# VectorE turns the probabilities of all four tiles, layernorm units later, four heads' scores and the second tile's rows moved

## The reference

```python
xn = layernorm(x)
q, k, v = (xn @ W + b  for each of q, k, v), as (blocks of 64 tokens, 8 heads, 128)
probs = softmax(q @ k.T * 128**-0.5)          # 64 x 64 for a head of a block
x = x + (probs @ v) @ Wo + bo
h = square(relu(layernorm(x) @ W_fc.T))
y = h @ W_proj.T
x = x + spikes(y) / 5                         # 5 steps of a leaky threshold: a count of y's levels
```

## Time and profile before

| | |
|---|---|
| median of 3 runs | 707.44 us (707.12 to 707.58) |
| the profiled execution's own time | 707.24 us |
| span of its slowest core (core 5), first to last instruction | 705.6 us |
| spans of the eight cores | 702.7 to 705.6 us |
| TensorE busy | 691.9 us, 98% |
| VectorE busy | 390.9 us, 55% |
| ScalarE busy | 179.7 us, 25% |
| granted TensorE clock, mean | 0.997 to 0.999 of full |

### The profile page before, as it was taken

One profiled execution on the slowest core, in us unless ns is written; L12 is line 12 of the kernel. 1 busy time (PEld: TensorE's weight loads), 2 busy tenths in 40 slices (PEclk: granted clock), 3 DMA queues, 4 the chain that ended last, 5 costly groups with the idle time before them and its releaser, 6 DMA issues.

```text
span 705.6 us, 10623 instructions; the slowest of 8 cores (702.7 to 705.6 us)
## 1 busy us (share of the span) xinstructions
PE 691.9 (98%) x3772; PEld 323.3 (46%) x3772; DVE 390.9 (55%) x589; ACT 179.7 (25%) x330; POOL 49.7 (7%) x96
## 2 busy tenths in 40 slices
PE   7999999999999999999999999999999999999996
PEld 3544444444444444444444444444444444444444
DVE  5327863776687488337655227845225865221476
ACT  3544550460351135130003331002331002332000
POOL 2211110211005000000000000000000000000000
PEclk9999999999999999999999999999999999999998
DMA  8998996598669995496461002272002152000011
GB/s 182 210 152 148 160 163 185 117 218 202 157 180 204 247 209 93 145 168 182 122 177 60 1 1 61 67 202 89 1 1 61 37 142 88 32 0 2 30 46 46
DMA packets 31012, 80.94 MB, mean 115 GB/s; under 512 B 5616, under 2 KB 5872, under 8 KB 30192
## 3 DMA queue, kind: packets, MB, share of 16 engines
q0 software_dynamic: 12960, 31.46, 26.0%
q1 hardware_dynamic: 15552, 40.39, 20.3%
q10 hardware_dynamic: 2448, 8.40, 3.0%
HBM read 82.33 MB, written 16.78 MB: 140 GB/s over the span
## 4 chain that ended last, share of the span: by engine, by line
PE 93%; DMA 4%; DVE 1%; issue 1%; POOL 0%; DVEq 0%; POOLq 0%
PE ps_m L439 31%; PE ps_y L517 30%; PE ps_m L386 13%; PE ps_m L412 8%; PE ps_m L426 8%; DMA wq_sb<-Wq 4%; DVE acc_sb L785 1%; PE ps_y L466 1%; PE ps_y L499 1%; PE ps_m L524 0%; PE ps_t L478 0%; DVE acc_sb L782 0%; DVE xr L790 0%; PE ps_t L368 0%; POOL wq_sb L879 0%
## 5 line engine op out<-in xcount | busy, mean ns | idle before, releaser
L439 PE MATMUL ps_m<-xn2t,w_sb 128*128 128x512 bf16 x1024 | 222.3, 379 | 0.0
L517 PE MATMUL ps_y<-w_sb,h_sb 128*128 128x512 bf16 (+1 forms) x1024 | 218.3, 376 | 0.0
L439 PEld LDWEIGHTS ps_m<-xn2t,w_sb 128*128 128x128 bf16 x1024 | 99.9, 98 | 120.1
L517 PEld LDWEIGHTS ps_y<-w_sb,h_sb 128*128 128x128 bf16 x1024 | 100.2, 98 | 117.6
L606 ACT ACTIVATE h_sb<-ps_m 128x512 bf16<-128x512 f32 x128 | 76.3, 597 | 263.4 <-PE ps_m L439 263.4
L775 DVE TENSOR_TENSOR h_sb<-h_sb 128x512 bf16<-128x512 bf16 x128 | 53.0, 424 | 121.5 <-ACT h_sb L606 121.3
L785 DVE SCALAR_TENSOR_TENSOR acc_sb<-ps_y,acc_sb 128x1024 bf16<-128x1024 f32 (+2 forms) x72 | 78.6, 1092 | 7.5
L386 PE MATMUL ps_m<-xnt,wq_sb 128*128 128x512 bf16 x240 | 56.8, 379 | 2.4 <-DMA wq_sb<-Wq 2.2
L386 PE MATMUL ps_m<-xnt,wk_sb 128*128 128x512 bf16 x248 | 58.6, 379 | 0.4 <-DMA wk_sb<-Wk 0.4
L412 PE MATMUL ps_m<-wv_sb,xnt 128*128 128x512 bf16 x256 | 56.6, 379 | 0.0
L426 PE MATMUL ps_m<-wo_sb,attn_sb 128*128 128x512 bf16 x256 | 55.9, 379 | 0.0
(11 more groups left out here) (66 smaller groups left out, 364.9 us busy)
## 6 DMA issues: line engine op xcount, KB each, us to landing
xr<-x SPq DMA_DIRECT2D x32, 512.0 KB, 7.3
xl<-x SPq DMA_DIRECT2D x96, 128.0 KB, 3.9
w_sb<-Wfc POOLq DMA_DIRECT2D x32, 256.0 KB, 9.8
x<-xr ACTq DMA_DIRECT2D x16, 512.0 KB, 5.2
out<-xr POOLq DMA_DIRECT2D x12, 512.0 KB, 2.9
w_sb<-Wpr POOLq DMA_DIRECT2D x16, 256.0 KB, 33.4
xn2t<-blk SPq DMA_DIRECT2D x64, 64.0 KB, 2.0
w_sb<-Wpr POOLq DMA_DIRECT2D x4, 1024.0 KB, 15.6
```

Source lines behind the costliest of these rows:

```text
L439: m = E.matmul(bank(key)[:], w1_sb[fc // 4][:, k0:k0 + 128], tokens(xn2t, c, 0, 4), start=(c == 0), stop=(c == 7))
L517: return E.matmul(out, h_sb[fc][:, tt * 128:(tt + 1) * 128], w2_sb[fc // 4][:, k0:k0 + n], start=(fc == 0), stop=(fc == 31))
```

## The change

Tiles 1 and 2 are treated as tiles 0 and 3 were: VectorE turns their probabilities (`p_turn`), TensorE's transposes and VectorE's copies of them go, and all tiles share one probability buffer and the layout of scores by blocks. In these blocks the turns move to slots 2, 6, 10, 13 and the values from slot 13 to 15 (in block 3 from 14 to 15). The wait ahead of a turn is now for the value matmuls that last read the same buffer. ScalarE copies the value projection out of PSUM in all blocks. The layernorm units start at slots 3, 12, 16, 20 in blocks 1 and 2, and at 5, 8, 10, 12 in block -1. The scores of tile 0's first four heads are issued at slot 10 of block -1, ahead of the queries of head 5, not at slot 0 of block 0. The loads of the second tile's rows each wait for one key weight more.

```diff
-BY_BLOCKS = (0, 3)
+FIRST_SCORES = (-1, 10)

 def scores_four(b, s):
-    return s // 8 if b >= 0 and s in (0, 8) else None
+    if (b, s) == FIRST_SCORES:
+        return 0, 0
+    return (b, s // 8) if b >= 0 and s in (0, 8) and (b, s) != (0, 0) else None

 def turn_p_pair(b, s):
-    slots = [2, 6, 10, 14 if b == 0 else 13] if b in BY_BLOCKS else [5, 9, 14, 17]
+    slots = [2, 6, 10, 14 if b == 0 else 13]
     return slots.index(s) if b >= 0 and s in slots else None

 def values_four(b, s):
-    slots = [16, 24] if b == 0 else [14 if b in BY_BLOCKS else 13, 18]
+    slots = [16, 24] if b == 0 else [15, 18]
...
+LN_FIRST = {-1: (5, 8, 10, 12), 0: (13, 17, 21, 25), 1: (3, 12, 16, 20), 2: (3, 12, 16, 20)}
...
 def ln_unit(b, s, step):
-    first, apart = {-1: (3, 3), 0: (13, 4)}.get(b, (3, 4))
-    n, rest = divmod(s - first - step, apart)
-    return 4 * (b + 2) + n if b <= 2 and rest == 0 and 0 <= n < 4 else None
+    firsts = LN_FIRST.get(b, ())
+    return 4 * (b + 2) + firsts.index(s - step) if s - step in firsts else None
...
-    p_sb = [at(f"p_sb_{i}", WORK + 57344 + 1024 * i, 512, BF16) for i in range(2)]
+    p_sb = at("p_sb", WORK + 57344, 512, BF16)
...
         def values(p, f):
-            E.wait_ge(*p_turned(p, 2 * f + 1))
+            E.wait_ge(ve_pt, 4 * p + 2 * f + 2)
...
-                if b not in BY_BLOCKS and (j := turn_p_pair(b, s)) is not None:
-                    turn_p(b, j)
-                if (f := scores_four(b, s)) is not None:
-                    scores(b, f)
+                if (which := scores_four(b, s)) is not None:
+                    scores(*which)
...
         # scalar_program
-                if b < 1 or key[0] != "v":
-                    main(key)
+                main(key)
...
         # vector_program, softmax_scale
-            if p in BY_BLOCKS and j > 0:
-                E.wait_ge(*p_turned(p, j - 1))
-            if p == 1 and j == 1:
-                E.wait_ge(full_v, 4)
+            if p + j > 0:
+                E.wait_ge(ve_pt, 4 * p + j)
...
         def p_turn(p, j):
             if p > 0:
-                E.wait_ge(full_v, 4 * p)
+                E.wait_ge(full_v, 4 * p - 2 + 2 * (j // 2))
...
-                    if b in BY_BLOCKS:
-                        p_turn(b, j)
-                    else:
-                        p_copy(b, j)
+                    p_turn(b, j)
...
-                if b > 0 and key[0] == "v":
-                    v_copy(key)
...
         # sync_program
         for i in range(4):
-            E.wait_ge(ld_wk[i], 16)
+            E.wait_ge(ld_wk[i + 1], 16)
             E.dma_start(out=xs[i][:], in_=rows(x_h, 4 + i)).then_inc(ld_xs[i], 16)
```

More of the change, by code:

```diff
@@ L160, in turn_order @@
                 keys.append(("x", i))
-            if b not in BY_BLOCKS and (j := turn_p_pair(b, s)) is not None:
-                keys.append(("pt", b, j))
     return {k: n for n, k in enumerate(keys)}
@@ L201, in build_nc @@
     attn_sb = at("attn_sb", ATTN_AT, 4096, BF16)
-    p_sb = [at(f"p_sb_{i}", WORK + 57344 + 1024 * i, 512, BF16) for i in range(2)]
-    pt_sb = [at(f"pt_sb_{i}", WORK + a, 512, BF16) for i, a in enumerate([59392, 60416, 58368, 96256])]
+    p_sb = at("p_sb", WORK + 57344, 512, BF16)
+    pt_sb = [at(f"pt_sb_{i}", WORK + a, 512, BF16) for i, a in enumerate([58368, 59392, 60416, 96256])]
     bo_sb = at("bo_sb", WORK + 61440, 1024, F32)
@@ L292, in emptied @@
         return free_m[main_no[key] % 3], main_no[key] // 3 + 1
[L294 to L309, removed]
     def values_bank(h):
@@ L462, in scores @@
                 E.wait_ge(*emptied(("k", p, h)))
-                for bl in sorted(range(8), key=lambda bl: scores_at(p, bl)):
-                    half, col = scores_at(p, bl)
-                    s0 = (h % 4) * 256 + col * 64
+                for bl in (0, 2, 4, 6, 1, 3, 5, 7):
+                    q0 = (bl % 2) * 64
+                    s0 = (h % 4) * 256 + (bl // 2) * 64
                     m = E.matmul(
-                        ps_s[half * 64:half * 64 + 64, s0:s0 + 64],
+                        ps_s[q0:q0 + 64, s0:s0 + 64],
                         q_sb[:, h * 512 + bl * 64:h * 512 + (bl + 1) * 64],
@@ L490, in values @@
                     kb = (bl % 2) * 64
-                    pt = pt_buffer(p, h // 2)[kb:kb + 64, :]
-                    if p in BY_BLOCKS:
-                        probs = pt.rearrange("p (b g t) -> p g b t", b=2, g=8)[:, (h % 2) * 4 + bl // 2, :, :]
-                    else:
-                        p0 = (h % 2) * 256 + (bl % 4) // 2 * 128 + (bl // 4) * 64
-                        probs = pt[:, p0:p0 + 64]
+                    g = (h % 2) * 4 + bl // 2
+                    pt = pt_sb[h // 2][:].rearrange("p (b g t) -> p g b t", b=2, g=8)
                     o0 = (bl % 2) * 512 + (h % 2) * 256 + (bl // 2) * 64
@@ L499, in values @@
                     m = E.matmul(values_bank(h)[:, o0:o0 + 64], v_sb[kb:kb + 64, v0:v0 + 128],
-                                 probs, start=True, stop=True)
+                                 pt[kb:kb + 64, g, :, :], start=True, stop=True)
                 if h % 2 == 1:
@@ L722, in softmax_scale @@
             E.wait_ge(ve_c, c)
-            if p in BY_BLOCKS and j > 0:
-                E.wait_ge(*p_turned(p, j - 1))
-            if p == 1 and j == 1:
-                E.wait_ge(full_v, 4)
-            E.tensor_tensor(p_buffer(p, j)[:].rearrange("p (g k) -> p g k", g=8), e8,
+            if p + j > 0:
+                E.wait_ge(ve_pt, 4 * p + j)
+            E.tensor_tensor(p_sb[:].rearrange("p (g k) -> p g k", g=8), e8,
                             rsum[:].unsqueeze(2).broadcast_to([128, 8, 64]),
@@ L732, in p_turn @@
         def p_turn(p, j):
-            blocks = p_buffer(p, j)[:].rearrange("p (g b t) -> p g b t", g=8, b=2)
-            turned = pt_buffer(p, j)[:].rearrange("p (b g t) -> p g b t", b=2, g=8)
+            blocks = p_sb[:].rearrange("p (g b t) -> p g b t", g=8, b=2)
+            turned = pt_sb[j][:].rearrange("p (b g t) -> p g b t", b=2, g=8)
             if p > 0:
-                E.wait_ge(full_v, 4 * p)
+                E.wait_ge(full_v, 4 * p - 2 + 2 * (j // 2))
             E.wait_ge(ve_p, 4 * p + j + 1)
@@ L746, in p_turn @@
             m.then_inc(ve_pt, 1)
[L748 to L756, removed]
         def add_bo(p, tt):
```

1 line of the change is left out of this document (removed).

## The result

| | before | after |
|---|---|---|
| median | 707.58 us (707.12 to 707.87) | 743.2 us (742.31 to 745.3) |
| span of the slowest core in the profiled execution | 705.6 (core 5) | 741.7 (core 6) |
| spans of all cores | 702.7 to 705.6 | 727.4 to 741.7 |
| TensorE busy | 691.9, 98% | 698.0, 94% |
| VectorE busy | 390.9 | 398.4 |

The ratio is 1.0504 (95% interval 1.049 to 1.0517): 36 us slower. Executions in which the cores of one die show a lower granted clock (one of the changed kernel's five, 835.77 us at 0.84) are left out everywhere, and since the chip of e1 to e4 had such a die with every kernel, for these four the slowest of cores 0 to 3 is given. Forecast were 720 and at most 727, so the sign is right and the size, with its range, is not.

What follows compares the result with a forecast made beforehand. TensorE's own gapless work from 38.10 to 692 us was taken as the bound. Sum: 707.24 - 1.5 (start) - 2.0 (transposes) + 6.3 (tile 3) + 10.0 (tile 4) = 720.0 us; range 708 to 727.

Steps and rivals of the forecast that it cites:

- Start: Kernel start: scores moved into the 1.5 us wait for query weights before head 5's queries; -1.5 us.
- Transposes: TensorE: eight groups of four probability transposes removed, 1.8 us, with the gaps at their seams -2.0 us.
- VectorE's load: Block 1: turns added on VectorE finish layernorm unit 13 at 153.5, 12.9 us later than before.
- The order of waits: Blocks 1 and 2: late unit 13 delays residual loads, bias additions, last block transpose, turning DMAs, then TensorE.
- Tile 3: Block 1's end: TensorE waits 4.8 to 7.7 us for the turned tile, middle 6.3.
- Tile 4: Block 2's end: same delay beside 16 weight loads, last turning DMA landing 7.2 later; wait of 10.0 us.
- The upper end: Tile 4: SyncE's 2.6 MB gets half of some 230 GB/s, takes 23 us; wait 13, sum 3 more.
- (A): Rival: transfers keep up, VectorE alone sets the end; 703.7 us, up to 706; chance 0.12.
- (B): Rival: only a part, residuals land as in block 2 before; +2 and +5.5, 711 us; chance 0.22.
- (C): Rival: turned probabilities late for the values, taken with the upper end's queue share; 722 to 728 us; chance 0.18.
- (D): Rival: change doesn't reach the path, SyncE not held by unit 13; gains and losses cancel, 706 to 709; chance 0.05.
- That the turned probabilities would be there for the values: Block 1: four pairs turned at about 153, TensorE wants them at 155; no wait, by 1 to 2 us.

Runs made afterwards that it cites:

- e1: Changed kernel with the layernorm units of blocks 1 and 2 back at slots 3, 7, 11, 15; 716.8 us on cores 0 to 3, +11.4.
- e4: Changed kernel, GpSimd's last two W1 loads and all of W2 held until tile 4 is turned; 717.5 us on cores 0 to 3.
- j1: Kernel before with each of TensorE's 32 transpositions of probabilities made twice; 709.26 us, ratio 1.0023.
- h4: Same kernel as e4 on another chip (late weight loads held until tile 4 is turned); 722.23 us, ratio 1.0204.
- k1: Changed kernel with ScalarE's four stores of block 2 held until tile 4 is turned; 735.81 us, ratio 1.0389.
- e2: Changed kernel with SyncE's four residual loads of a block moved ahead of the rows; 731.2 us on cores 0 to 3.
- h1: Same kernel as e1 on another chip (changed kernel, layernorm units at the slots of before); 718.12 us, ratio 1.0146.
- i1: h1 with ScalarE's square root of a unit issued behind its copy of the slot's group, not ahead; 720.26 us, ratio 1.0188.
- i2: i1 with the square roots of blocks 1 and 2 one slot later still; 727.36 us, ratio 1.0281.
- h3: Kernel before with only its layernorm units of blocks 1 and 2 at slots 3, 12, 16, 20; 727.35 us, ratio 1.0274.
- both parts: Later layernorm units alone on the kernel before (h3), +19.4 us; turned probabilities alone (h1, less the start's -1.3), +11.6 us.
- holding kernels: Versions with late weight loads, in some also ScalarE's stores, held until tile 4 is turned; among them h4 1.0204, g1 1.0209, k2 1.0013.
- k2: Changed kernel with third row buffer, residuals first, last units at 16 and 19, later bias additions, some weight loads and block 2's stores held; 708.64 us, ratio 1.0013.
- g1: Changed kernel with third row buffer, residuals first, last units at 16 and 19, later bias additions, late weight loads held; 722.86 us, ratio 1.0209.

## Why the prediction was wrong

**What held.** Start: -1.5 forecast, -1.3 measured alone; in the profiled execution of the changed kernel its slowest core shows nothing of it (block 1 begins at 121.8), as there the weights of head 6 were 1.2 us late. Transposes: -2.0 forecast, 1.6 by j1. VectorE's load: unit 13 scaled by 153.5 forecast, 155.1 measured (the forecast is the end of the scaling, 12.9 after 140.6), 1.6 late:

```profile
154.25 0.81 DVE L665 TENSOR_SCALAR xn<-xl,mv,rstd 128x1024 bf16<-128x1024 f32 x1
```

The order of waits, residual loads, last block transposition, turning, landing, is the forecast one in both blocks.

**Tile 3: 6.3 forecast, 9.9 measured** (8.8 longer, with 1.0 of transposes gone). The third residual was issued 1.5 later than forecast, for those 1.6 of VectorE's, and took 14.28, not 13.2; turning began at 176.4, not 173.6. Its 16 issues took 11.7 us to the last, not 9.8 (one of them 2.03), and the last landed in 2.1, at the lower end of "2.0 to 4.9". 2.8 + 1.9, less 1.3 against the middle of the landings, make 3.4 of the 3.6 missing. As forecast, part of it shows as TensorE's stop in the output projection.

**Tile 4: 10.0 forecast, 26.8 measured. This is the step that failed**: "With the landing of block 1 (third residual 13.2) the turn starts at the same distance, and its last DMA lands 7.2 later". Counted from block 2's first query group, the turning began 7.5 us later than that: 5.2 by the residual (18.4 for 13.2) and 2.1 because it was issued later. Unit 17's scaling began 33.7 us after that group, forecast 30.3, in block 1 31.8; SyncE made up 1.3 of the 3.4. Of the 2 us that block 2 has over block 1, 1.6 come from the clock: the first exponentials stand on ScalarE behind the copy of the first query group, and this group took 3.44 us for 1.89. TensorE's group, and what VectorE waited, 5.53 us where in block 1 it was 1.77:

```profile
190.47 3.44 PE L371 MATMUL ps_m<-xnt,wq_sb 128*128 128x512 bf16 x8 [2.15 <-DMA xnt<-blk]
...
195.32 0.69 DVE L689 TENSOR_REDUCE ssum<-e_sb 128x8 f32<-128x512 f32 x1 [5.53 <-ACT e_sb L582]
```

Then the landing, 8.5 (15.7 for 7.2), 0.4 in the issues and 0.5 from the landing to TensorE's first matmul: 7.5 + 8.5 + 0.4 + 0.5 = 16.9, against 16.8 missing. Both large terms were read from rows with another company: 13.2 from block 1, where GpSimd issued four weight pieces ahead of it and four within its landing (139.64 and 154.58); 7.2 from turning DMAs with weight loads beside them, all issued ahead of ScalarE's stores. Against block 2's first query group the turning moved later by 22.7 us (217.57 less 181.56, and 249.17 less 190.47), the stores only by 12.4 (230.51 and 251.86). That moved it onto the stores, which the prediction never named. h4 takes both landings down (21 us back), k1 the stores' part of the last (8 back), e2 VectorE's waits for residuals in both blocks (6.5 back). The prediction also counted 16 weight loads in block 2; there are 24, the last eight issued at 236.76, 12 us ahead of the turning.

**The upper end** was worked out for the residuals alone (half of 230 GB/s, 23 us; they took up to 20.5) and kept 7.2 behind it; the sum by the Trainium skill's rule of queues taken in turn (DMA: Bandwidth & Descriptors, "Queues, rings and completion order"), 3 more, fell 14 us short of the wait at tile 4 as well. No run tells that rule from another.

**The clock.** No term was there for it. Granted clock by stretches of core 6 (us, TensorE busy and count, clock, DMA share, GB/s):

```profile
190.00:194.00 4.00, 3.53 (x10) 0.57 0.43 117
...
250.00:264.00 14.00, 11.35 (x72) 0.82 1.06 256
...
268.00:277.00 9.00, 1.44 (x4) 0.50 1.04 242
277.00:300.00 23.00, 23.00 (x131) 0.96 0.57 118
```

0.50 is the lower of the two levels, 1.2 GHz; the clock is lowered in the stops and still low for some matmuls behind them. The first query group took 3.44 us, not 1.89, and the first 64 matmuls of the up projection 15.64, not 13.97: 3.2 us in all, the 1.5 behind the first up projection among them and the first query group's inside the 26.8. The slow matmuls of block 2's output projection (40 in 10.63 us, for 8.79 in block 1) lie inside the wait for tile 4. Not every wait has this price: behind the wait of 2.9 us for tile 4 on h1's core 5 the 64 took 13.97, and behind one wait of 2.12 us in h1 a group took 1.89 us on core 5 and 3.57 on core 0. No run here tells why.

**The rivals.** (A), transfers keep up, is refuted by the waits; (B) was much too mild. (C), forecast at 722 to 728, had turned probabilities late for the values: with the units moved this happened in neither block. With the units where they were, h1, i1 and i2 show value matmuls that wait for VectorE, 2.2 to 6.5 us, but for its reading of the scores. (D) is refuted by h3. That the turned probabilities would be there for the values, by 1 to 2 us, held nearly: by 0.9 us in block 1 (154.2, values at 155.1) and 0.5 in block 2.

**What stays open.** The 6 us by which both parts exceed their sum weren't taken apart. The holding kernels show that a version can have the change and lose next to nothing (k2), but the two gains never came out on top: k2's slowest core still waited 2.6 us for head weights at the start, 1.1 for tile 3 and 0.8 for tile 4. Why the landing of a 64 KB DMA rises with stores and weight loads together and not with stores alone is measured, not explained.

## What to carry to other kernels

Moving a producer's steps later in a block moves every DMA queued behind them, and each lands by what is in flight at its new time: list all issuers of that time, the stores of other engines too, before borrowing a landing time from a row. Ask of an engine at 55% of the span whether it has any room in the stretch where work is added; here VectorE had none, and the room made for it by moving the layernorm cost more than the transposes it took over. A wait of TensorE can be longer than itself: behind the 12.9 us here some matmuls ran at half speed and cost 1.7 us more, behind h1's 2.9 us none did.

## What was not expected of the hardware

64 KB turning DMAs land in 2.0 to 3.3 us beside 0.5 MB stores alone (h4), in 5.4 to 10.5 beside 256 KB weight loads (k1, k2), and in up to 15.7 beside both (the changed kernel, core 6; 17.5 on core 7). And weight loads held for some 27 us (from about 210, where the kernel before issues them, to 237 in g1) were not made up for: with the DMA engines' share at 0.9 to 1.1 from 236 to 320, W2's pieces took up to 60 us to land, in the kernel before up to 40.
